# A four-layer recurrent stage whose stream is kept centred, with its phases ordered anew

## What is computed

```python
h = x @ Win.T + bin                      # 512 -> 64
for each of 4 layers:
    y = silu(layernorm(h, l1w, l1b))
    y = sconv(y, phazor, last_conv)      # a complex recurrence along the 1024 tokens, real part
    h = h + y * scl
    y = layernorm(h, l2w, l2b)
    y = silu(y @ w1.T + b1)              # 64 -> 256
    h = h + y @ w2.T + b2                # 256 -> 64
s = layernorm(h, lnl_w, lnl_b) @ Wout.T + bout    # 64 -> 512
```

## Time and profile before

| | us |
|---|---|
| median of 3 runs | 705.05 (704.93 to 705.63) |
| profiled execution | 706.01 |
| its span in the trace | 704.0 |
| second block: from its start to the end of the span | 469.1 to 704.0 |
| phase 0, up to the h of half 1 | 469.1 to 509.0 |
| phase 1 | 509.0 to 530.9 |
| phases 2 to 7 | 530.9 to 651.8 |
| the last 10 gate steps | 651.8 to 659.1 |
| phases 8 and 9, up to the last DVE instruction | 659.1 to 701.5 |

### The profile page before, as it was taken

The page is one execution under the profiler, slowest core; times in us unless marked ns, Lnnn a source line. Parts: engine busy times, 40 slices in busy tenths (PEclk is TensorE's granted clock), DMA queues, the critical chain, the costliest instruction groups (busy, mean ns, idle before and its releaser), DMA issues. The chain is left out here.

```text
span 704.0 us, 8644 instructions
## 1 busy us (share of the span) xinstructions
PE 630.7 (90%) x2788; PEld 455.8 (65%) x2788; DVE 488.1 (69%) x936; ACT 330.4 (47%) x551; POOL 172.1 (24%) x296
## 2 busy tenths in 40 slices
PE   5788999999999999999999998967398889899874
PEld 4676878888888888888888885654144444334432
DVE  6797897877877877877877866767545545554145
ACT  5679285285285285285285284213243333433220
POOL 1000001001001001001001039944434555423134
PEclk9999999999999999999999999988799999999897
DMA  8711002002002002002001036001000000000033
GB/s 300 274 41 61 0 1 90 1 2 89 0 0 89 0 0 89 0 0 89 0 0 61 1 113 224 2 20 43 0 1 0 1 0 1 0 0 1 0 120 119
DMA packets 17181, 32.32 MB, mean 46 GB/s; under 512 B 3224, under 2 KB 3736, under 8 KB 17152
## 3 DMA queue, kind: packets, MB, share of 16 engines
q1 hardware_dynamic: 17152, 31.97, 13.0%
HBM read 24.62 MB, written 7.34 MB: 45 GB/s over the span
## 5 line engine op out<-in xcount | busy, mean ns | idle before, releaser
L750 DVE TENSOR_SCALAR_CACHE_REDUCE junk_d<-k_buf,cand 128x1376 int8<-128x1376 f32 x56 | 91.8, 1640 | 0.3
L581 ACT ACTIVATE junk_a<-k_buf,cand 128x1376 int8<-128x1376 f32 x56 | 80.5, 1437 | 0.6
L1014 PE MATMUL ps_a<-wd_hi,zt_hi 128*128 128x512 f32 (+1 forms) x176 | 71.8, 408 | 2.0 <-DVE zt_lo L863 1.0
L562 ACT ACTIVATE s_buf<-ps_a 128x1376 f32<-128x1376 f32 x16 | 21.1, 1319 | 106.0 <-PE ps_a L987 103.6
L1014 PE MATMUL ps_a<-wd_hi,zt_lo 128*128 128x512 f32 (+1 forms) x176 | 69.2, 393 | 0.0
L1014 PE MATMUL ps_a<-wd_lo,zt_hi 128*128 128x512 f32 (+1 forms) x176 | 68.9, 392 | 0.0
L1642 PE MATMUL ps_b<-arena,xt 128*128 128x512 f32 x128 | 65.5, 639 | 0.0
L503 POOL TENSOR_TENSOR xres<-xres,gate 128x512 f32<-128x512 f32 x12 | 23.6, 1965 | 144.5 <-DVE gate L870 144.5
L495 POOL TENSOR_TENSOR rstd<-var_eps,expo 128x2 f32<-128x2 f32 x8 | 5.6, 706 | 204.1 <-DVE var_eps L691 204.1
L987 PE MATMUL ps_a<-wg_hi,xt_hi 128*128 128x512 f32 (+1 forms) x192 | 53.2, 386 | 2.0 <-DVE xt_lo L679 2.0
L987 PE MATMUL ps_b<-wu_hi,xt_hi 128*128 128x512 f32 (+1 forms) x192 | 52.3, 381 | 0.0
(11 more groups left out here) (212 smaller groups left out, 1307.1 us busy)
## 6 DMA issues: line engine op xcount, KB each, us to landing
xin<-in_x SPq DMA_DIRECT2D x8, 512.0 KB, 3.6
xres<-in_x SPq DMA_DIRECT2D x8, 512.0 KB, 3.5
out<-arena SPq DMA_DIRECT2D x16, 256.0 KB, 2.0
x_scratch<-xres SPq DMA_DIRECT2D x6, 512.0 KB, 3.0
arena<-x_scratch SPq DMA_DIRECT2D x3, 1024.0 KB, 12.6
m_buf<-in_wd_t SPq DMA_DIRECT2D x3, 512.0 KB, 9.5
m_buf<-in_wg_t SPq DMA_DIRECT2D x2, 688.0 KB, 5.3
k_buf<-in_wg_t SPq DMA_DIRECT2D x2, 688.0 KB, 7.8
```

Of the source, the lines that this page charges most:

```text
L562: act.activation(s_buf[:, t, :], ps_a[:].rearrange("p a n -> p (a n)")[:, 0:INNER], ACT.Silu).then_inc(s_ready, 1)
L581: act.activation(junk_a[:], k_buf[:, 1, :], ACT.Sign, bias=c, scale=-1.0, accum_out=below[:, 1:2]).then_inc(act_step, 1)
L750: dve.tensor_scalar(junk_d[:], k_buf[:, 0, :], c, -float(DROP), ALU.is_lt, ALU.add, accum_out=e).then_inc(cnt_dve, 1)
L1014: last = pe.matmul(ps_a[:, t, :], zs, ws[0:rows, c, :], start=(c == 0 and n == 0), stop=(c == CHUNKS - 1 and n == 2))
```

## The change

1. **The stream is kept centred.** DVE takes the mean over the 64 features out of the in-projection weights `win` and the second feed-forward weights `w2` once (`center_weights`), and PE out of the biases `bin` and `b2` (`center_biases`). What the in-projection and the feed-forward part put into h then has mean zero. The layernorm before a mixing (q even) and the last one need no `center_rows`: `squares` and `normed` read h itself. After the recurrence h is not centred, so the layernorm before a feeding (q odd) still has one, and `centered` now writes its result back to h.
2. **`GATES`** is (1, 2, 1, 3, 2, 1): still 10 steps a phase, in six places. 10 steps more stand in phase 0, none after phase 7. ACT's `gate(2 * phase)` and the second one stand elsewhere and take tiles two further on.
3. **`tables`** are spread in twos: two at the start of the phases 2 to 6 on POOL, the others in phase 0; before, in threes at the end of the phases 0 to 5.
4. **The first phase.** PE's `tokens` no longer wait for POOL's constants. DVE takes its four tiles first, then splits the bias rows, then applies tokens. The statistics of the last four tiles stand around `variance`.
5. **The last phases.** Phase 8 has outputs 0 to 3 between its up and down units, phase 9 has outputs 4 to 7 ahead of and inside its layernorm, then 8 to 15. Before, outputs 0 to 7 all stood in phase 8.

The core of the diff:

```diff
-GATES = (2, 3, 1, 3, 1)
+GATES = (1, 2, 1, 3, 2, 1)
@@ POOL
                 root_tokens(2)
-                tables(0, 0, 6)
+                tables_some(0, 6)
                 root_tokens(3)
-                for phase in range(PHASES):
+                tables_some(6, 8)
+                root(0, 0)
+                tables_some(8, 10)
+                pool.wait_ge(tb, N_SMALL + 6)
+                times_sin(0, 0, y, ln_o, 1, cv_wi)
+                times_sin(0, 0, u_im, cv_ui, 1, cv_b)
+                pool.wait_ge(h_ready[0], 2)
+                tables_some(10, 14)
+                for phase in range(1, PHASES):
...
+                    if phase > 1 and l < DEPTH:
+                        pool.wait_ge(h_ready[c], 2 * l + 1)
+                        tables_some(10 + 2 * phase, 12 + 2 * phase)
                     root(2 * l, c)
@@ ACT
                 def squares(q, c):
-                    act.wait_ge(ln_cent[c], q + 1)
-                    act.activation(sq[:, cs(c)], bank1[c], ACT.Square).then_inc(ln_sq[c], 1)
+                    if q % 2:
+                        act.wait_ge(ln_cent[c], q // 2 + 1)
+                    else:
+                        act.wait_ge(h_ready[c], q + 1)
+                    act.activation(sq[:, cs(c)], bank1[c] if q % 2 else h[:, cs(c)], ACT.Square).then_inc(ln_sq[c], 1)
...
-                    elif l < DEPTH:
-                        gate(2 * phase - 2)
                     if l < DEPTH:
+                        gate(2 * phase)
                         norm_out(q, c, ACT.Silu, pcol(l, C_L1W), pcol(l, C_L1B))
...
-                            if u == 1 and l < DEPTH:
-                                gate(2 * phase - 1)
+                            if u == 2 and l < DEPTH:
+                                gate(2 * phase + 1)
@@ DVE
+                def center_weights(w, at, n, loaded, count, done):
+                    mean = off[:, at:at + n]
+                    dve.wait_ge(loaded, count)
+                    dve.tensor_reduce(mean, w, AX_X, ALU.add).then_inc(done, 1)
+                    dve.wait_ge(done, 1)
+                    dve.tensor_scalar(mean, mean, -1.0 / DIM, None, ALU.mult).then_inc(done, 1)
+                    dve.wait_ge(done, 2)
+                    dve.tensor_tensor(w, w, mean.rearrange("p (n o) -> p n o", o=1).to_broadcast([P, n, DIM]),
+                                      ALU.add).then_inc(done, 1)
...
                     if phase == 0:
+                        center_weights(w2[:], KH, 2 * DEPTH, w2_in, 16, w2_s)
                         h_in(1)
@@ PE
+                variances(0, 0)
+                pe.wait_ge(rows_lo, 3)
+                pe.wait_ge(xt_a, 8)
+                gates(1)
+                spread(0, 0)
+                gates(KH)
+                for i in range(12, TILES):
+                    tokens(i)
+                project_in(1)
+                gates(KH + 1)
+                for phase in range(1, PHASES):
...
                     if feeds:
                         center_rows(n, d)
+                    else:
+                        pe.wait_ge(f_free, FF * DEPTH)
+                        output(4)
+                        output(5)
+                    gates(fill[0])
```

More of the change, by code:

```diff
@@ L1406, in _ @@
                 act.activation(ones_r[:], ones[:], ACT.Copy).then_inc(rows_lo, 1)
-                for phase in range(PHASES):
+                act.wait_ge(rows_left, 1)
+                for r in (32, 96):
+                    act.activation(row_r[r:r + 1, :, :], row_f[r:r + 1, :, :], ACT.Copy).then_inc(rows_lo, 1)
+                squares(0, 0)
+                for i in range(PER_HALF, PER_HALF + 4):
+                    take_tile(i)
+                act.wait_ge(par_in, 16 * 4)
+                norm_out(0, 0, ACT.Silu, pcol(0, C_L1W), pcol(0, C_L1B))
+                for i in range(PER_HALF + 4, TILES):
+                    take_tile(i)
+                gate(0)
+                gate(1)
+                for phase in range(1, PHASES):
                     l, c = mixing(phase)
                     k, d = feeding(phase)
-                    feeds = 0 < phase < PHASES - 1
+                    feeds = phase < PHASES - 1
                     q, n = 2 * l, 2 * k + 1
@@ L1436, in _ @@
                             hidden(k, d, u)
-                            if u == 1 and l < DEPTH:
-                                gate(2 * phase - 1)
-                    if phase == PHASES - 3:
-                        for t in range(2 * phase, TILES):
-                            gate(t)
+                            if u == 2 and l < DEPTH:
+                                gate(2 * phase + 1)
             @block_b.vector
@@ L1557, in _ @@
                     q, n = 2 * l, 2 * k + 1
-                    outs = range(PER_HALF * c, PER_HALF * (c + 1)) if l == DEPTH else ()
-                    variance(q, c)
-                    if feeds:
-                        variance(n, d)
-                    widen(q, c)
-                    normed(q, c)
-                    if feeds:
-                        widen(n, d)
-                        normed(n, d)
+                    if phase == PHASES - 1:
+                        output(4)
+                        output(5)
+                    if phase:
+                        variance(q, c)
+                        if feeds:
+                            variance(n, d)
+                        if phase == PHASES - 1:
+                            residual(3)
+                            output(6)
+                            output(7)
+                        widen(q, c)
+                        normed(q, c)
+                        if feeds:
+                            widen(n, d)
+                            normed(n, d)
                     if l < DEPTH:
@@ L1677, in output @@
                               start=False, stop=True).then_inc(o_ps, 1)
-                pe.wait_ge(mk, N_MK)
-                for i in range(8):
-                    tokens(i)
-                project_in(0)
-                tokens(8)
-                tokens(9)
                 steps = iter(range(TILES * (KH + 1)))
@@ L1688, in gates @@
                     for _ in range(n):
-                        i = next(steps, None)
-                        if i is not None:
-                            gate_step(i)
-                for phase in range(PHASES):
+                        gate_step(next(steps))
+                for i in range(8):
+                    tokens(i)
+                center_biases()
+                project_in(0)
+                for i in range(8, 12):
+                    tokens(i)
+                variances(0, 0)
[5 more added lines that the diff above has]
+                for i in range(12, TILES):
+                    tokens(i)
+                project_in(1)
+                gates(KH + 1)
+                for phase in range(1, PHASES):
                     l, c = mixing(phase)
                     k, d = feeding(phase)
-                    feeds = 0 < phase < PHASES - 1
+                    feeds = phase < PHASES - 1
+                    fill = GATES if l < DEPTH else (0,) * len(GATES)
                     q, n = 2 * l, 2 * k + 1
-                    outs = range(PER_HALF * c, PER_HALF * (c + 1)) if l == DEPTH else ()
-                    center_rows(q, c)
-                    if phase == 0:
-                        tokens(10)
-                        tokens(11)
-                        variances(q, c)
-                        tokens(12)
-                        tokens(13)
-                        spread(q, c)
-                        tokens(14)
-                        tokens(15)
-                        project_in(1)
-                        pe.wait_ge(rows_lo, 3)
-                        continue
                     if feeds:
                         center_rows(n, d)
-                    gates(GATES[0])
+                    else:
+                        pe.wait_ge(f_free, FF * DEPTH)
+                        output(4)
+                        output(5)
+                    gates(fill[0])
                     variances(q, c)
```

176 lines of the change are left out of this document (105 added, 71 removed).

## The result

The changed kernel takes 686.92 us, median of 3 runs (684.98 to 687.82), against 705.05 before: 0.975 of the time before [0.972, 0.978]. The forecast was 680.5 with a range of 674 to 687, so the time lies at the upper edge of the range. Direction and most of the size were right; 24.3 us were forecast and 18.1 came. One term of the sum failed, by 3.0 us.

The account below looks back on a forecast made before the run. In steady phases DVE's strand was taken to end last, with PE, the busiest engine, idle 1.66 us before the next centring. Terms -8.8, -7.3, -1.0, -2.4, -4.8 sum to -24.3: 705.05 to 680.75, said 680.5, range 674 to 687.

Parts of the forecast that it names:

- The step that failed: Phase 1, the first after phase 0: 19.5 us instead of 21.9, a term of -2.4 us.
- The last gate steps: Ten gate steps, PE alone after phase 7, move into PE's idle time in phase 0: -7.3 us.
- Phases 2 to 7: Steady phases: five of 18.5 us, phase 7 17.8, plus 1.8 for two at lower clock; 112.1 against 120.9, -8.8.
- The layout: Steady phase timed from F, the end of `fed`: ACT's gate released at F + 8.2, `turn` at F + 9.8.
- handing over the carry: Steady phases, between `turn` and the end of `into_h`: costs 0.9 us more, so F + 17.6 instead of F + 16.7.
- Phase 0 and the end: Phase 0: h of half 1 at 508.0, -1.0 us; phases 8 and 9: 19.3 and 18.3 us, -4.8.
- The first: Rival: gate's wait and tables ahead of the root eat the gain, phases stay 19.8 us; 688 us, chance 0.08.
- The second: Rival: the clock falls once in each of seven phases, +5 to +8 us, about 687; chance 0.10.
- The third: Rival: waits in the steady phases cost less than laid out, 17.4 us a phase; 674 us, chance 0.10.
- The fourth: Rival: PE at 1.2 GHz through whole phases, about 34 us each; two such give 710 us; chance 0.03.
- The rule against the change: Steady phases: PE alternating bursts and waits among small matmuls could lose the clock in every phase; the rows showed two of seven.
- that nothing hides: Phase 0, `center_weights` of `w2` on DVE ahead of `h_in` of half 1: 2.0 us taken as fully exposed.

## Why the prediction was off, point by point

**The step that failed** is phase 1: "One phase of 18.5, plus 1.0 for gate steps still queued: 19.5. Term: -2.4." Phase 1 took 22.5. The steady phase of 18.5 was right; the term for queued gate steps was mis-sized, and the clock was put at nothing. The five moved steps behind the second in-projection are not the rest of a queue that runs dry in 1.0 us. They are a whole gate tile, 4.1 us, ahead of the centring in PE's list, and cost 3.2 us (22.5 to 19.3 with them earlier; with ACT's gate alone moved, nothing). The other 0.8 is the lower clock, 0.91 to 0.92 in phase 1 with the steps or without: 18.5 + 3.2 + 0.8 = 22.5. The prediction took PE's 9.04 us of idle time in the earlier trace rows as room for all ten steps. That piece lay behind an in-projection that was done at 500.10. In the changed kernel the in-projection ends at 507.78, so the idle piece moved ahead of the first spread, and five of the ten steps stand behind it.

**The last gate steps**: -7.3 came as forecast at the end. But the term was booked as if free, and its price lies in phase 1: net 3.3.

**Phases 2 to 7**: -8.0 for -8.8. The layout held in the main: the gate started at F + 8.0 to 8.2 at full clock and F + 8.8 to 8.9 at the lower one (8.2 forecast), `turn` at F + 9.4 to 10.3 (9.8), and `fed` waited for PE. The 0.9 us for handing over the carry did not come. `into_h` ended at F + 16.9 in phase 2, which hands over (17.6 forecast), and at F + 17.6 in phase 3, which does not (16.7), and what tells the two apart is the clock: at 1.00, with the ten steps last, phase 3 gave 16.9 as well. At full clock a phase took 18.3 to 18.5, as forecast. Phase 7 without tables took 19.25 where 17.8 was forecast, but the clock was down in it; at full clock, with the ten steps last, it took 17.94. The clock fell in three of the six where two were counted, and the three falls cost 2.7 us by the run with the ten steps last, for 1.8 booked.

**Phase 0 and the end**: -1.2 for -1.0, and -4.6 for -4.8, both partly by luck. In phase 0 `turn` came at 499.81, or 498.7 with the block's later start taken off, 1.4 after the forecast 497.3. The recurrence behind it took 6.5 us (499.81 to 506.27) instead of 8.8. The prediction's own sum gave 508.8, and it said 508.0; measured, with the start taken off, were 507.8. For `center_weights(w2)` 2.0 us were taken, and 2.1 measured. At the end phase 8 took 18.6 us for 19.3 and phase 9 19.2 for 18.3, and the two misses nearly cancel.

**The rivals.** The first (phases stay at 19.8 us) is refuted: none of the phases 2 to 7 took more than 19.5 in either trace of the changed kernel. The second (the clock falls in every phase) came true half: in phases 1, 3, 5 and 7, at 0.7 to 1.3 us each. Its 687 is near the time measured, but not by its cause. With the failed step alone put right the forecast is 680.5 + 3.0 = 683.5; 0.8 came from the phases 2 to 7, 1.1 from the later start of the block, 0.96 because the execution profiled before stood that much above its median while the one after was its median, and 0.25 was rounded off (680.75 to 680.5). The clock's part beyond what was forecast is 0.8 in phase 1 and 0.9 in the phases 2 to 7. The third (the waits cost less) needed the gate out of the way, and then gave 17.8 and not 17.4, with PE busy for 17.0 to 17.2 of it. The fourth (slower) is refuted.

**The rule against the change.** Three of the six steady phases lost the clock, phase 1 beside them, and with another order of the same steps none of the six did. The rows of before already had three of seven at 0.90 to 0.92, phase 1 among them, where the prediction counted two. The Trainium skill, "TensorE: Matmul & The Clock Gate", section "HAM oscillation — how this bites in real kernels", says that alternating bursts and waits can lose the clock again in each round. The trace agrees for the phases 8 and 9, where filling PE's waits raised the clock from 0.72 and 0.82 to 0.90 and 0.94 and brought 3.8 us, and not for the steady phases, where it was lost in every second round or in none.

## What to carry to other kernels

Work moved into an idle stretch of an engine is free only if it stands ahead of the instruction on which the next stage waits: look up where in the list each moved step lands, and book its price there, not where it left. The idle stretch of the old trace may itself have moved: here it went from behind the in-projection to ahead of the first spread. A wait taken off one strand is worth the distance to the next strand (here 1.7 us gave 0.7, since PE's own list ended the phase), and a 2 us piece "that nothing hides" gave nothing. Where matmuls are small and spaced, try several orders and some filler work: 0.7 to 1.7 us a phase hung on the granted clock alone.

## What was not expected of the hardware

The granted clock alternated from phase to phase (1.00, 0.91, 1.00, 0.91 ...) in a loop whose phases are alike on PE, and did so again in a second set of runs. With the ten steps back at the end it alternated the other way round, down in the phases 2, 4 and 6. Reordering the ten gate steps of a phase, with the same 61 matmul records and less idle time, held it at 1.00 in all six phases, in two kernels. Moving three DVE operations in phase 0 cost the clock in phase 2 (0.91, 1.6 us) with PE's list unchanged, in both kernels that had the edit. What decides it between these orders was not isolated and stays open.
